# Order of TensorE's work in the first attention: products, scores and transposes of a step side by side

## The reference

```python
# x: rmsnorm(layernorm(x)) for the queries; ctx for keys and values; 32 heads of 128
h_q = (x @ w_q.T).reshape(b, lq, 32, 128)
h_k = (ctx @ w_k.T).reshape(b, lk, 32, 128)
h_v = (ctx @ w_v.T).reshape(b, lk, 32, 128)
score = einsum('bqhd,bkhd->bhqk', h_q, h_k) + position_bias[None]
score = softmax(where(m, score, -inf)); score = where(m, score, 0)
attn = einsum('bhqk,bkhd->bqhd', score, h_v).reshape(b, lq, 4096)
out = hidden_states + attn @ w_out.T          # then x + tanh(g) * out
```

## Time and profile before

| | |
|---|---|
| time, median of 3 runs | 1711.79 us (1711.14 to 1712.65) |
| the profiled execution's own time | 1710.41 us |
| its span | 1708.3 us |
| PE busy | 1625.9 us (95%) |
| PE weight loads busy | 1290.6 us (76%) |
| DVE busy | 958.2 us (56%) |
| ACT busy | 743.0 us (43%) |
| POOL busy | 347.9 us (20%) |
| mean granted TensorE clock | 0.988 |

### The profile page before, as it was taken

How to read it: one execution, slowest core, us unless ns; L and a number is a source line. 1 busy time by engine, 2 the same in 40 slices (tenths; PEclk the granted TensorE clock), 3 DMA queues, 4 the chain that set the end, 5 groups by cost and what they waited for, 6 DMA issues and landing times.

```text
span 1708.3 us, 26003 instructions
## 1 busy us (share of the span) xinstructions
PE 1625.9 (95%) x8984; PEld 1290.6 (76%) x8984; DVE 958.2 (56%) x2491; ACT 743.0 (43%) x2174; POOL 347.9 (20%) x241
## 2 busy tenths in 40 slices
PE   7999999999999999999998999999999899999975
PEld 6888888888888888888765869686876797555554
DVE  5552534525345253452577757667576757577687
ACT  4542443424434244342423544536363231776642
POOL 3210212102121021210025000000004433243352
PEclk9999999999999999999999999999999999999988
DMA  5111101111011110110440000000016022000001
GB/s 182 53 41 41 48 28 52 40 41 48 28 52 40 45 44 28 52 40 25 136 171 19 8 13 0 12 0 0 1 38 210 26 66 73 1 13 13 1 1 49
DMA packets 34134, 76.04 MB, mean 45 GB/s; under 512 B 5537, under 2 KB 18337, under 8 KB 31905
## 3 DMA queue, kind: packets, MB, share of 16 engines
q1 hardware_dynamic: 34080, 75.36, 13.2%
HBM read 73.25 MB, written 2.10 MB: 44 GB/s over the span
## 4 chain that ended last, share of the span: by engine, by line
PE 69%; DVE 15%; ACT 8%; issue 4%; DVEq 2%; POOL 1%; DMA 0%; POOLq 0%; ACTq 0%; SPq 0%
PE banks L956 14%; PE banks L966 10%; PE banks L1051 10%; PE banks L1154 9%; PE banks L1258 5%; PE banks L1230 3%; PE banks L1022 3%; ACT p L867 3%; DVE sA L1571 3%; PE banks L1037 2%; ACT sA L663 2%; PE banks L1364 2%; PE banks L1357 1%; PE banks L1029 1%; DVE sA L1583 1%
## 5 line engine op out<-in xcount | busy, mean ns | idle before, releaser
L1594 DVE TENSOR_TENSOR x_res<-banks,x_res 128x512 f32<-128x512 f32 x120 | 82.9, 691 | 207.6 <-PE banks L1051 207.2
L956 PE MATMUL banks<-cT,w_k 128*128 128x512 f32 x720 | 179.8, 398 | 0.0
L966 PE MATMUL banks<-w_v,cT 128*128 128x512 f32 x768 | 179.7, 392 | 0.0
L956 PE MATMUL banks<-xT,w_q 128*128 128x512 f32 x720 | 175.4, 396 | 0.0
L1051 PE MATMUL banks<-w_o,atT 128*128 128x512 f32 x720 | 169.9, 392 | 2.2 <-DVE x_res L1594 2.0
L663 ACT ACTIVATE sA<-sA,nmA 128x128 f32<-128x128 f32 x256 | 99.3, 390 | 166.5 <-DVE nmA L1571 165.6
L966 PEld LDWEIGHTS banks<-w_v,cT 128*128 128x128 f32 x768 | 142.7, 188 | 28.9
L1051 PEld LDWEIGHTS banks<-w_o,atT 128*128 128x128 f32 x720 | 133.7, 188 | 31.6 <-DVE x_res L1594 2.9
L956 PEld LDWEIGHTS banks<-xT,w_q 128*128 128x128 f32 x720 | 131.9, 188 | 25.5
L956 PEld LDWEIGHTS banks<-cT,w_k 128*128 128x128 f32 x720 | 130.8, 188 | 25.2
L1578 DVE TENSOR_SCALAR rsA<-smA 128x4 f32<-128x4 f32 x64 | 15.8, 247 | 185.4 <-ACT sA L663 185.4
(11 more groups left out here) (241 smaller groups left out, 3231.9 us busy)
## 6 DMA issues: line engine op xcount, KB each, us to landing
w_raw_k<-in_w0k SPq DMA_DIRECT2D x16, 512.0 KB, 3.3
w_raw_v<-in_w0v SPq DMA_DIRECT2D x8, 1024.0 KB, 7.4
w_raw_q<-in_w0q SPq DMA_DIRECT2D x15, 512.0 KB, 3.3
w_raw_o<-in_w0o SPq DMA_DIRECT2D x15, 512.0 KB, 3.3
cTp<-in_ctxT SPq DMA_DIRECT2D x12, 512.0 KB, 3.8
wq_raw<-in_wq SPq DMA_DIRECT2D x1, 3072.0 KB, 10.3
wo<-in_wo SPq DMA_DIRECT2D x1, 3072.0 KB, 20.0
kT<-in_ctxT SPq DMA_DIRECT2D x4, 512.0 KB, 6.8
```

The costliest lines, as they stand in the source:

```text
L956: mm = pe.matmul(dst, w[l][:, c, h * P:(h + 1) * P], t[r][:, c, half * 512:(half + 1) * 512], start=n == 0, stop=n == 3 * DC - 1)
L966: mm = pe.matmul(dst, cT[l][:, c, b * P:(b + 1) * P], wv_[r][:, c, :], start=n == 0, stop=n == 3 * DC - 1)
L1594: dve.tensor_tensor(x_res[:, b, :], bank(6 + b % 2), x_res[:, b, :], ALU.add).then_inc(S("o_added"), 1)
```

## The change

Two things are reordered, with the same instructions. On TensorE, attend(g) moves behind the second of the two projection units of a step, so that attend(g), scores(g+2) and turn(g+1) follow one another; in odd pairs the last attend moves behind unit 9. On ACT, the store of that second unit moves ahead of `store_at`, and the rounding of v and of q, which stood ahead of `store_pT`, now stands behind it. DVE's, GpSimd's and SyncE's programs are the same.

```diff
@@ ScalarE, head_pair @@
                 unit(2)
                 exps(p, 1)
+                unit(3)
                 store_at(p, 0)
-                unit(3)
+                store_pT(p, 1)
                 if ahead and par == 0:
                     round_w("v", quad)
-                store_pT(p, 1)
                 unit(4)
                 exps(p, 2)
+                unit(5)
                 store_at(p, 1)
-                unit(5)
+                store_pT(p, 2)
                 if ahead:
                     round_w("q", p + 1)
-                store_pT(p, 2)
                 unit(6)
                 exps(p, 3)
+                unit(7)
                 store_at(p, 2)
-                unit(7)
                 store_pT(p, 3)
                 if par == 1:
                     unit(8)
+                    unit(9)
                 store_at(p, 3)
-                if par == 1:
-                    unit(9)
@@ TensorE, head_pair @@
                 turn(0)
                 proj_unit(2)
+                proj_unit(3)
                 attend(0)
-                proj_unit(3)
                 scores(2)
                 turn(1)
                 proj_unit(4)
+                proj_unit(5)
                 attend(1)
-                proj_unit(5)
                 scores(3)
                 turn(2)
                 proj_unit(6)
+                proj_unit(7)
                 attend(2)
-                proj_unit(7)
                 turn(3)
                 if par == 1:
                     proj_unit(8)
+                    proj_unit(9)
                     attend(3)
-                    for u in range(9, QK_UNITS + V_UNITS):
+                    for u in range(10, QK_UNITS + V_UNITS):
                         proj_unit(u)
```

## The result

The changed kernel takes 1722.8 us, median of six runs (1720.53 to 1723.57), against 1711.33 us for the kernel before in the same six rounds (1709.17 to 1712.65): ratio 1.0066, 95% interval 1.0056 to 1.0076. It is slower, by 11.5 us; +11.1 us and 1722.9 us were forecast. The profiled execution took 1721.83 us, its span is 1719.8 us, again 11.5 us over that of before.

The account below looks back on a forecast made before the run. TensorE was taken as the bound, its matmuls running 830.2 of 837.0 us. Seven times an even pair's +1.86 and an odd pair's -0.27 gave +11.1 us, hence 1722.9 us; range 1715 to 1729, the forecast's own 1720 to 1726.

Parts of the forecast that it names:

- Grouping worth nothing: TensorE's steps: putting units two and two leaves a step at 7.71 us, taken as 0, at most +-1.4 us.
- Step 1, T2: Even pair: v subtraction starts 1.31 us later, holds norm(2) longer, and turn(2) on TensorE waits 1.31 us.
- The hold: DVE's operations from SBUF to SBUF don't run during GpSimd's subtraction; norm(2) held 1.31 us longer, bounds 0 to 4.6.
- Step 2, q behind the reductions: Even and odd pairs: q subtraction starts just after scores(3)'s last reduction, by 0.3 and 0.25 us, so its hold goes.
- Step 3, the out products: Even pair: out products wait for late attend(2), its store and rest(2); TensorE waits 1.09 us, 0.5 us added.
- The pairs: Loop's seven even and seven odd head pairs: even 1.86 us longer, odd 0.27 us shorter, +11.1 us together.
- The first: Rival, norm(2) in even pairs: the hold is not one, turn(2) doesn't wait; +1.6 us, 1713.4 us; 6%.
- The third, a near miss that hits: Rival, odd pairs: q subtraction starts 0.25 us earlier and holds the last reduction; 6 us more, 1729 us; 8%.
- The fourth, the clock: Rival, even pairs: TensorE's clock falls in the new gaps, +12 us if each gets one, 1735 us; 5%.
- The second: Rival, both pairs: faster, as rest(2) or the waits at turn get hidden; 1708 us; 4%.

Follow-up runs that it names:

- e5: Changed kernel with v rounded and subtracted at the even pair's end, and even pairs' attend(2) ahead of unit 7 again: 1707.52 us, ratio 0.9977.
- e10: Kernel before, TensorE's order kept, with ACT rounding q behind the copy of pT(2) and v at the even pair's end: 1707.71 us, ratio 0.9976.
- e3: Changed kernel with rounding and subtraction of v moved to the even pair's end, under the out products: 1714.05 us, ratio 1.0019.
- e6: Kernel before, TensorE's order kept, with only ACT's rounding of v moved behind the copy of pT(1): 1719.27 us, ratio 1.005.
- e9: Changed kernel with GpSimd's 128x2048 subtraction for v cut into four of 128x512: 1720.65 us, ratio 1.0062.
- e4: Changed kernel with even pairs' attend(2) ahead of unit 7 again on TensorE, and its store ahead of unit 7's on ACT: 1716.28 us, ratio 1.0033.
- e1: Changed kernel with ACT rounding v ahead of the copy of pT(1) again: 1728.83 us, ratio 1.0108.
- e7: Changed kernel with ACT rounding q ahead of the copy of pT(2) again: 1748.25 us, ratio 1.0216.

## Why the prediction was right

- **The total.** The medians agree within 0.1 us by luck, as three small terms cancel: the kernel before was 0.5 us faster in these six rounds than in the three that the forecast started from, the loop cost 0.5 us less than forecast, and 0.9 us came from outside it.
- **Grouping worth nothing.** 7.70 us a step against 7.71 forecast, and 0.07 us per two pairs between e5 and e10. The bound of +-1.4 us was generous.
- **Step 1, T2.** 1.31 us forecast, 1.27 measured; e3 takes it out, e6 puts it in alone. The hold was read from one 0.87 us row whose end fell on the end of a GpSimd row: it cost nothing in the kernel before, as T2 followed S3 there after the usual 0.89 us (293.94 to 294.83), with next to nothing to spare. That is the step on which the forecast turned, and it is shown, and so is what the description at the start leaves out: the engines' programs meet only at semaphores, but a GpSimd operation holds one of DVE's without any. Two things in the reading were too wide. The rule for all of DVE's operations from SBUF to SBUF doesn't hold for the reciprocal of e9. And the addition of scores(3) did lie under the start of a subtraction before the change (295.27 to 295.95, subtraction from 295.76), at no cost; in e6 additions and rest run 0.68 us wholly under the q subtraction. The small difference: the subtraction itself is 4.58 us here and 4.63 in the earlier trace rows, where a reduction was in work when it began.
- **Step 2, q behind the reductions.** From the start of the last reduction to that of the subtraction 0.3 us were forecast in the even pair and 0.25 in the odd; measured are 0.40 (301.56 to 301.96) and 0.26 (344.76 to 345.02). In the odd pair this reduction was still in work when the subtraction began, and took its normal 0.28 us. It fell on the right side in every pair, with little room. T3's wait 0.20 forecast, 0.19 measured (306.70 against 305.62 + 0.89). The 0.26 us that the prediction sets beside it is a bracket; from start to start T3 waited 0.42 us before (302.12 - 298.88 - 2.82). Its sum is not touched, as it was made from starts.
- **Step 3, the out products.** T3 to out products 1.45 us forecast, 1.46 measured; e4 takes 0.8 us of it out.
- **The pairs.** Even +1.86 forecast, +1.80 measured; odd -0.27, -0.28. Of 11.1 us forecast for the loop 10.6 came; the profiled span's 11.5 holds another 0.9 us. 0.5 of it lie ahead of the first pair's scores (59.47 against 58.94 us) and are not the change's: matmuls of 512 columns start every 0.43 us at first and every 0.23 later, and this step came at 12.9 us before the change and at 13.9 in the changed kernel (15.7 in e4, where the first scores start at 60.41). Behind the loop are 0.3 us, of which 0.1 is the change's. For the even pair there the prediction said 0, with A3 waiting for the copy of pT(3) as before; it is 32.11 us long and was 32.02, and its A3 (847.50, idle 0.83) now waits for DVE's rest(2), the chain of step 3.
- **Rivals.** The first is ruled out by e3 and e6. The third, a near miss that hits, didn't happen here. e1 shows on the v subtraction what it would have been, a last reduction held for a whole subtraction. e7 is no test of it: there the q subtraction began 1.3 us earlier, caught the first reduction in odd pairs (2.13 us long), and cost them 0.25 us. The fourth, the clock, didn't happen with gaps of 1.3 and 1.1 us and did in e7 with 3.2 us. The second was off for two reasons, the chain behind A2, which it gives, and T2's hold: taking out one of them still leaves the kernel slower than before (e3, e4), without both it is 3.7 us faster (e5).

## What to carry to other kernels

When an instruction order is changed, follow not only who waits for whom but which engine's long operation lands on whose short ones: here a rounding on ACT moved 1.3 us, with it a GpSimd subtraction, and a DVE operation that takes 0.17 us when free, and took 0.87 before, took 2.14 on TensorE's path. A held operation in the profile that costs nothing is the first thing to look for before moving anything near it, and the operation that holds has to be followed past every DVE operation it can meet, not just the next. TensorE's grouping was the visible part of this change and worth nothing; one of the two best versions (1702 and 1703 us, not told apart) keeps the old order of TensorE and moves only when ACT and GpSimd do their work.

## What the runs showed of the hardware that was not expected

- Behind an idle TensorE of 3.24 us the clock fell to 0.50 (its lower level, 1.2 GHz) for 3.4 us or more in five of seven even pairs of e7; behind one of 1.95 us, in e1, in two of seven; behind 1.10 and 0.81 us, in the loop of the changed kernel, never. Each stretch of 3.4 us cost about 1.6 us (an even pair of e7 is 48.08 us with one and 46.48 without).
- The v subtraction reads 4.74 us in e1, where a DVE reduction had just begun as it started, against 4.58 in the changed kernel, where it met none. Smaller differences say nothing: it is 4.63 before the change, where a reduction was in work, but also 4.62 in e3, where none was.
- DVE's operations that read PSUM are not held: additions take 0.69 us under the subtractions for v (e3) and k (changed kernel), additions and rest 0.68 us under that for q (e6).
- The hold goes by GpSimd's instruction, and not every DVE operation takes part: in e9 a multiplication gets in between two quarters, and the reciprocal runs 0.18 us inside one.
